# Quarter of the gram evacuation to VectorE, its additions to GpSimd, and another order of loads and weights, in a fused pairwise-interaction MLP

## What is computed

```python
dots = einsum('bfd,bgd->bfg', bottom_output, bottom_output)
pairs = dots[:, TRIL_I, TRIL_J]                 # 351 per sample
x = concatenate([bottom_mlp_output, pairs, zeros], axis=1)     # 480
for w, b in ((w0, b0), (w1, b1), (w2, b2), (w3, b3)):          # 1024, 1024, 512, 256
    x = relu(x @ w.T + b)
return x @ w_out.T + b_out
```

## Time and profile before

| | us |
|---|---|
| median of 3 runs | 570.56 |
| lowest and highest run | 570.14, 571.0 |
| profiled execution, its span from first to last instruction | 570.2 |
| PE busy (share of the span) | 542.0 (95%) |
| ScalarE busy | 340.8 (60%) |
| VectorE busy | 330.0 (58%) |
| GpSimd busy | 10.8 (2%) |

### The profile page before, as it was taken

One profiled execution on the slowest core, in us unless ns is written; L12 is line 12 of the kernel. 1 busy time (PEld: TensorE's weight loads), 2 busy tenths in 40 slices (PEclk: granted clock), 3 DMA queues, 4 the chain that ended last, 5 costly groups with the idle time before them and its releaser, 6 DMA issues.

```text
span 570.2 us, 13265 instructions
## 1 busy us (share of the span) xinstructions
PE 542.0 (95%) x4457; PEld 531.7 (93%) x4457; DVE 330.0 (58%) x941; ACT 340.8 (60%) x900; POOL 10.8 (2%) x58
## 2 busy tenths in 40 slices
PE   4768799999999999999999999999999999999997
PEld 3667799999999999999999999999999999999996
DVE  3778678727872488427872488427872488425222
ACT  4988479827971499317971499417981399414112
POOL 1500000000000000000000000000000000000000
PEclk9977899999999999999999999999999999999999
DMA  7987324044304141232304131222304131200000
GB/s 222 260 233 223 89 65 117 12 104 124 109 16 119 37 121 47 61 87 78 109 11 112 43 116 53 62 87 77 109 7 111 47 115 56 55 22 1 1 1 0
DMA packets 89898, 47.32 MB, mean 83 GB/s; under 512 B 25851, under 2 KB 88083, under 8 KB 89875
## 3 DMA queue, kind: packets, MB, share of 16 engines
q1 hardware_dynamic: 89874, 47.02, 29.5%
HBM read 41.03 MB, written 5.98 MB: 82 GB/s over the span
## 4 chain that ended last, share of the span: by engine, by line
PE 73%; ACT 12%; DMA 6%; issue 5%; SPq 2%; DVE 0%; ACTq 0%; DVEq 0%
PE acc L551 61%; ACT parts L641 9%; PE gram_ps L518 6%; PE turned_ps L502 5%; DMA rows<-in_r_bottom_output_dram 5%; ACT xt L624 2%; ACT h_full L654 1%; DMA blocks<-grams 1%; PE gram_ps L485 1%; SPq L366 1%; SPq L355 1%; SPq L344 1%; DMA pairs<-blocks 1%; PE turned_ps L564 0%; PE turned_ps L527 0%
## 5 line engine op out<-in xcount | busy, mean ns | idle before, releaser
L551 PE MATMUL acc<-h_a,w_hi 128*128 128x256 f32 x1152 | 211.2, 283 | 0.9 <-ACT h_full L654 0.8
L654 ACT ACTIVATE h_full<-acc,small_t 128x256 f32<-128x256 f32 x176 | 83.2, 473 | 183.2 <-PE acc L551 181.5
L551 PEld LDWEIGHTS acc<-h_a,w_hi 128*128 128x128 f32 x1152 | 179.2, 191 | 2.2 <-ACT h_full L654 2.2
L641 ACT ACTIVATE parts<-gram_ps 27x216 f32<-27x216 f32 x512 | 173.4, 339 | 5.9 <-PE gram_ps L518 1.1
L551 PE MATMUL acc<-h_a,w_lo 128*128 128x256 f32 x576 | 163.0, 283 | 0.0
L551 PEld LDWEIGHTS acc<-h_a,w_lo 128*128 128x128 f32 x576 | 110.4, 192 | 0.0
L551 PE MATMUL acc<-x,w_hi 128*128 128x256 f32 (+1 forms) x512 | 98.5, 289 | 3.7 <-DVE x L806 3.7
L518 PE MATMUL gram_ps<-xt 128*128 128x256 f32 x512 | 95.9, 312 | 1.0 <-ACT parts L641 0.7
L551 PE MATMUL acc<-h_b,w_hi 128*128 128x256 f32 x512 | 93.3, 284 | 0.0
L736 DVE TENSOR_TENSOR xt<-turned_ps,xt 128x432 fp32r<-128x432 f32 x128 | 77.3, 604 | 18.7 <-ACT xt L624 15.7
L502 PE MATMUL turned_ps<-ident,rows 108*128 108x108 f32 x512 | 72.8, 267 | 16.0 <-DMA rows<-in_r_bottom_output_dram 15.1
(11 more groups left out here) (54 smaller groups left out, 346.3 us busy)
## 6 DMA issues: line engine op xcount, KB each, us to landing
rows<-in_r_bottom_output_dram SPq DMA_DIRECT2D x128, 216.0 KB
blocks<-grams SPq DMA_DIRECT2D x32, 182.2 KB
stage_b<-in_L_rec_w_dram SPq DMA_DIRECT2D x2, 1024.0 KB, 9.6
stage_b<-in_L_rec_w_dram SPq DMA_DIRECT2D x1, 2048.0 KB, 7.8
stage_a<-in_L_rec_w_dram SPq DMA_DIRECT2D x1, 1536.0 KB, 11.5
stage_pairs<-in_L_rec_w_dram SPq DMA_DIRECT2D x1, 1408.0 KB, 9.7
mlp_rows<-r_bottom_mlp_output_dram SPq DMA_DIRECT2D x8, 128.0 KB, 2.2
pairs<-blocks SPq DMA_DIRECT2D x8, 126.0 KB
```

The source lines that it names most:

```text
L551: last = nc.tensor.matmul(acc_slot(slot), weight(wp, layer, m, k), in_tile(layer, k, xp), start=(k == 0 and n == 0), stop=(k == K_TILES[la ...
L641: last = nc.scalar.activation(parts[quad, u % 2, :, :, 0:FEATS], gram_ps[quad, b:b + GRAM_BANKS, :].rearrange("p a (b h n) -> p h (a b) n" ...
L654: nc.scalar.activation(h_full[:, slot % 2, :], acc_slot(slot), ACT.Relu, bias=small_t[:, slot:slot + 1]).then_inc(drained, 1)
```

## The change

- Of a unit's four quadrant copies ScalarE keeps three (`ACT_QUADS`), VectorE does the fourth (`last_part`). VectorE keeps the 32 by 32 transpose (`turn_low`); GpSimd does both additions (`add_parts`).
- The pairs are held in the order of W0's columns, so no column is moved. The gather has 28 pieces, each of one feature's rows; the DRAM scratch is laid out by quadrant, so the spill writes whole rows of `grams` and a gathered pair row is four runs of 64 numbers. Chunk 0's pieces are issued half by SP and half by ScalarE, after its fifth group of weights; later chunks' all by SP. The pair tiles have a semaphore each.
- The raw weights lie where `w_lo` will be and are split in place. The groups go in the order W0, small, W1, W2, W3. Nine are turned ahead of chunk 0, none of them between units. Chunk 0 has a hook every six matmuls (`FIRST_HOOK`): the first sixteen take W1, then come the units of chunk 1, and from unit 4 on a group of W2 or W3 stands behind each of ten units. These ten use the `turned_ps` bank that the next unit's transposes use, which wait for the group's `w_done`.
- Chunk 0's rows have sixteen places of their own or nearly so (eight share memory with `h_b`, four are the ring, four are used twice), and are loaded with 112 instead of 108 partitions. Ten loads go out ahead of W0.
- Chunk 0's products wait for the groups that they need, tile by tile.

```diff
-BETWEEN_UNITS, FIRST_BETWEEN = 8, 7
+ORDER = W0_ALL + SMALL + W1_ALL + W2_ALL + W3_ALL
+BEFORE_CHUNK, LATE_WEIGHTS = ORDER.index(W1_ALL[0]), ORDER.index(W2_ALL[0])
-HOOK = 9
+HOOK, FIRST_HOOK = 9, 6
+GATHER_AFTER, LATE_FROM = 4, 4
+ACT_QUADS = 3
+def first_hooks():
+    hooks, late = groups(BEFORE_CHUNK, LATE_WEIGHTS), groups(LATE_WEIGHTS, W_GROUPS)
+    for u in range(UNITS + XT_LAG):
+        hooks.append(unit_steps(u))
+        if u >= LATE_FROM and late:
+            hooks.append(late.pop(0))
+    return hooks + late
...
         def weight_bank(n):
-            if n < BETWEEN_UNITS:
-                return acc[:, n % ACC_RING, :]
+            if n >= LATE_WEIGHTS:
+                return turned_ps[:, (LATE_FROM + n - LATE_WEIGHTS + 1) % TURN_RING, :]
             return gram_ps[:, n % (GRAM_RING * GRAM_BANKS), :]
+        def gather_piece(engine, a, b, n, q):
+            dst = pairs[q % P:q % P + n, q // P, :].rearrange("p (s r) -> p s r", s=GROUP)
+            engine.dma_start(dst, pair_rows[a, b:b + n]).then_inc(gathered[q // P], 16)
...
                 for s in range(GROUP):
-                    sp.dma_start(blocks[:, :, s * RUN:(s + 1) * RUN],
-                                 grams[QUAD * s:QUAD * s + FEATS, :, :]).then_inc(spilled, 16)
+                    sp.dma_start(blocks[s], grams[quad_of(s)]).then_inc(spilled, 16)
...
+            for u in range(10):
+                load_early(u)
+            for i in range(2):
+                sp.dma_start(raw_rows(0)[:, 4 * i:4 * i + 4, 0:LAYERS[0][0]], w0_rows[:, 4 * i:4 * i + 4, :]).then_inc(w0_loaded[i], 16)
+                load_early(10 + i)
+            for u in range(12, UNITS):
+                load_early(u)
             load_mlp(0)
...
+            for i in range(2):
+                load_weights(1, w1, 2 * i, 2 * i + 2, w1_loaded[i])
             spill(0)
+            gather(0, PIECES[0::2])
+            for i in range(2, 4):
+                load_weights(1, w1, 2 * i, 2 * i + 2, w1_loaded[i])
             for u in range(ROWS_RING):
                 load_rows(1, u)
+            for i in range(2):
+                load_weights(2, w2, 2 * i, 2 * i + 2, w2_loaded[i])
+            load_weights(3, w3, 0, 2, w3_loaded)
...
-            for col, n, q, step in ROW_RUNS:
-                nc.gpsimd.tensor_copy(w0_ordered[:, :, q:q + (n - 1) * step + 1:step], stage_pairs[:, :, col:col + n])
+            def add_parts(d, u):
+                n = d * UNITS + u + 1
+                hh, hl = parts[:, u % 2, 0], parts[:, u % 2, 1]
+                pool.wait_ge(parts_done, n)
+                pool.wait_ge(last_part_done, n)
+                nc.gpsimd.tensor_tensor(hh, hh, hl, ALU.add).then_inc(sum_done, 1)
+                pool.wait_ge(sum_done, n)
+                pool.wait_ge(low_turned, n)
...
+                nc.gpsimd.tensor_tensor(
+                    grams[:, :, u * UNIT_GROUPS:(u + 1) * UNIT_GROUPS].rearrange("p g j -> p j g"),
+                    parts[:, u % 2, 0, :, 0:FEATS], low_t[:, u % 2, :, 0:FEATS], ALU.add).then_inc(grams_done, 1)
...
             def turn_weights(n):
+                elif n >= LATE_WEIGHTS:
+                    pe.wait_ge(xt_done, UNITS + LATE_FROM + n - LATE_WEIGHTS)
...
             def turn(d, u):
+                if isinstance(d, int) and d == 1 and LATE_FROM < u <= LATE_FROM + W_GROUPS - LATE_WEIGHTS:
+                    pe.wait_ge(w_done, LATE_WEIGHTS + u - LATE_FROM)
...
             def gram_parts(d, u):
-                for s in range(GROUP):
+                for s in range(ACT_QUADS):
+                    last = nc.scalar.activation(parts[quad_of(s), u % 2, :, :, 0:FEATS], gram_found(u, s), ACT.Copy)
                 last.then_inc(parts_done, 1)
...
+            def last_part(d, u):
+                dve.wait_ge(gram_done, d * UNITS + u + 1)
+                for s in range(ACT_QUADS, GROUP):
+                    last = nc.vector.tensor_copy(parts[quad_of(s), u % 2, :, :, 0:FEATS], gram_found(u, s))
+                last.then_inc(last_part_done, 1)
```

More of the change, by code:

```diff
@@ L143, in first_steps, with groups, chunk_steps @@
         steps += unit_steps(u)
[L144 to L163, removed]
+    steps.append(("mlp",))
+    for n in range(BEFORE_CHUNK):
+        steps.append(("weights", n))
+        if n == GATHER_AFTER:
+            steps.append(("gather",))
+    return steps + [("pairs",)]
+def first_hooks():
+    def groups(n0, n1):
+        return [[("weights", n)] for n in range(n0, n1)]
+    hooks, late = groups(BEFORE_CHUNK, LATE_WEIGHTS), groups(LATE_WEIGHTS, W_GROUPS)
[4 more added lines that the diff above has]
+    return hooks + late
+def chunk_steps(gram, first=False):
+    steps, done = [], 0
+    hooks = first_hooks() if first else [unit_steps(u) for u in range(UNITS + XT_LAG)] if gram else []
+    every = FIRST_HOOK if first else HOOK
+    hooks.reverse()
     for layer in range(3):
@@ L176, in chunk_steps @@
                 done += 3 * n
-                if layer < 2 and done % HOOK == 0:
-                    hook()
-                if done == OUT_UNIT * HOOK:
+                if layer < 2 and done % every == 0 and hooks:
+                    steps.extend(hooks.pop())
+                if done == OUT_UNIT * every:
                     steps.append(("out",))
@@ L481, in turn_weights @@
                     if part == 0:
                         pe.wait_ge(loaded, 16)
-                    for k in range(4):
-                        at = (4 * part + k) * P
-                        last = nc.tensor.transpose(bank[:, k * P:(k + 1) * P], src[:, at:at + P], ident[:])
-                last.then_inc(w_turned, 1)
+                src = raw_rows(layer)[:, m, :]
+                for k in range(4):
+                    kk = K_LAST if layer == 0 and k == 3 else P
+                    at = (4 * part + k) * P
+                    last = nc.tensor.transpose(bank[0:kk, k * P:(k + 1) * P], src[:, at:at + kk], ident[:])
@@ new lines, in turn_weights, with turn_rows, turn_early @@
+                last.then_inc(w_turned, 1)
+            def turn_rows(u, src):
+                for j in range(UNIT_GROUPS):
+                    last = nc.tensor.transpose(turned_ps[:, u % TURN_RING, j * GROUP_ROWS:(j + 1) * GROUP_ROWS],
+                                               src[0:GROUP_ROWS, j, :], ident[0:GROUP_ROWS, 0:GROUP_ROWS])
+                last.then_inc(turned, 1)
+            def turn_early(u):
+                pe.wait_ge(early_loaded[u], 16)
+                if u >= TURN_RING:
+                    pe.wait_ge(xt_done, u + 1 - TURN_RING)
+                turn_rows(u, early_rows_of(u))
```

282 lines of the change are left out of this document (126 added, 156 removed).

## The result

| | before | after |
|---|---|---|
| median, us | 570.35 (4 runs) | 583.95 (4 runs) |
| lowest and highest run | 568.98, 571.0 | 583.55, 585.17 |
| profiled execution, span | 570.2 | 581.8 |
| ScalarE / VectorE / GpSimd busy | 340.8 / 330.0 / 10.8 | 305.9 / 325.7 / 115.5 |

The changed kernel takes 1.025 times as long, interval 1.0232 to 1.0268. The forecast was 577.0 in a range of 567 to 589: slower was right, by 6.6 us forecast and 13.6 measured.

A forecast was written before the change was run, and what follows sets the result against it. PE bounds the steady chunks; ahead of chunk 0 it waits for rows and a serial chain to the pairs. 570.2 - 14.3 + 7.7 + 11.5 + 3.4 + 1.0 - 2.4 = 577.1, given as 577.0, range 567 to 589.

The forecast's parts named there:

- The road to the pairs of chunk 0: Ahead of chunk 0: faster units, spill and gather bring the first pairs product to 48.2 from 62.55 us, gain 14.3.
- the two roads to the pairs: Ahead of chunk 0: the gather with the last tile's work, and ScalarE's issues then four weight groups, both end at 48.2.
- rival 1: Chunk 0: ScalarE's and VectorE's copies run ahead of PE, the bank waits' 11.5 us fall away, 565.5 us; chance 0.16.
- rival 2: Gather: pieces cost 0.79 us each, delaying chunk 0, chunk 1 and each later chunk, 610 us; chance 0.08.
- rival 3: First stage: GpSimd's two additions set the pace at about 2.0 us a unit, +6, 583 us; chance 0.12.
- the ten bank waits: Chunk 0: PE waits for turned_ps banks used by W2 and W3 groups, 5 x 0.85 + 5 x 1.45 = +11.5 us.
- the wait before chunk 1: End of chunk 0: PE is through at 89.1, chunk 1's pairs are ready at 92.5, so it waits 3.4 us.
- the start value of the sum: Whole kernel: the sum starts from the profiled span, 570.2 us, with no correction to the median of 570.56.
- chunk 0 without the wait behind it: Chunk 0: 18 more weight groups (+7.7 us) and the bank waits (+11.5) lengthen it from 69.9 to 89.1 us.
- slow clock in chunk 1: Start of chunk 1: a slower PE clock after the wait for its pairs adds 1.0 us.
- five steady chunks and the last: Later chunks: ScalarE's gaps give back 0.4 us in each of six, -2.4 us; bounds 0 and 0.9 each.
- rival 4: Chunks' layer 0: GpSimd and VectorE block each other, 0.25 us over in ten hooks of six chunks, +15, 592; chance 0.05.

The follow-up runs named there:

- experiment 8: Changed kernel with ScalarE's fourteen gather issues for chunk 0 behind all nine groups of W0 and small vectors instead of the first five: 583.34 us.
- experiment 1: Changed kernel with the ten W2 and W3 groups right behind W1's, in the gram banks, and the units of chunk 1 after them: 571.7 us.
- experiment 2: Changed kernel with the ten W2 and W3 groups behind the units of chunk 1, in the gram banks: 567.89 us.
- experiment 4: Changed kernel with both additions back on VectorE, which also keeps the fourth quadrant's copy: 623.59 us.
- experiment 3: Kernel before with only the new division of gram work among ScalarE, VectorE and GpSimd, from chunk 1's grams on: 565.29 us.
- experiment 6: Changed kernel with the early loads of chunk 0's rows on 108 partitions instead of 112: 583.72 us.

## Why the prediction was right and wrong

**Right.** The road to the pairs of chunk 0, all of it by its steps: ScalarE's unit 1.53 to 1.60 us (1.50 forecast), spill issued at 33.6 (34.0), landed 5.2 us later (5.5), pieces at 0.40 from start to start (0.38 in the sums), first product on pairs 48.3 (48.2). In one place the steps may not hold: the forecast let the two roads to the pairs end together, and experiment 8 points to ScalarE's as the later one. GpSimd's additions 0.47 and 0.43 (0.5). PE stood before all of the ten turns named, released by w_lo, and before chunk 1, released by the last pair tile and the drain behind it. Experiments 1 and 2 show that these waits are the loss, and the first of them gives their price: 12.2 us. No rival came about: the fastest bank wait was 0.95 us (rival 1 needed 0.67 on the mean), in chunk 1's gather one piece of 28 took 0.89 us, the first 0.57 and the others 0.24 to 0.42 (rival 2), GpSimd was far under 1.5 us a unit (rival 3).

**Wrong, by 7.0 us.** Every wait stood where it was forecast; the sizes were wrong. The step that failed most is the price of the ten bank waits, put at 11.5 us and measured at 14.0; behind it stand the wait before chunk 1, which came out of a wrong boundary of chunk 0, and the start value of the sum. The ledger runs over the profiled spans, before and after, which differ by 11.5 us where the terms summed to 6.9:

| term | forecast | measured |
|---|---|---|
| start of chunk 0's pairs | -14.3 | -14.23 |
| chunk 0 without the wait behind it | +19.2 | +22.70 |
| wait before chunk 1 | +3.4 | +4.74 |
| slow clock in chunk 1, with what that chunk gains | +1.0 | +1.64 |
| five steady chunks and the last (forecast: six times 0.4) | -2.4 | -3.34 |

1. *The ten bank waits.* "Sum 5 x 0.85 + 5 x 1.45 = +11.5" was 14.0: PE stood 1.56 us the first time, 1.72 to 1.74 in the five with a drain and 0.95 in the other four. Three things add up to the 2.5 us. From VectorE's last result to PE's next start it is 0.15 us (79.04 to 79.19), where the sum had 0.05: 1.0 over ten waits. The first wait, without a drain, had ScalarE still on the unit's three parts: 0.6. And in each of the five with a drain the cast on VectorE, which the subtraction and the weights' rest stand behind, took 0.48 to 0.49 us instead of 0.29, while GpSimd's first addition ran (81.74 and 81.86 in the timeline): that is the 0.9 left. In experiment 4, where GpSimd adds nothing, no cast takes over 0.30. That is 2.5 of the 3.5 us in the second line. Another 0.6 is the half clock: 10.3 us of it around chunk 0's start, 4.6 us of work at half speed inside the chunk and so 2.3 us lost, where the forecast kept the 1.7 of the earlier trace rows. The last 0.4 us has no row of its own.

2. *The boundary of chunk 0.* "Chunk 0 itself takes 69.9 us" was read between 62.2 and 132.1, but chunk 1's first product stood at 130.4: the 132.1 was nine products and a turn into it. In the sum of differences that cancels, except in one place. "PE is through at 89.1, so it waits 3.4" sets one end counted from single durations (92.5) against one counted from the 69.9. With 68.1 PE is through at 87.3 and waits 5.2, and that is 1.8 us more in the sum. The measured 4.7 has two errors that nearly cancel: both the pairs and PE's end came 3 to 4 us later than that.

3. *"The span of the profiled execution is 570.2 us, the median of the runs shown 570.56, nothing worth a correction."* This compared a span with a whole time. In the 22 runs of the kernel before beside experiment 1, the time is 2.5 us longer than the span and the median span is 567.75. So the profiled execution of before was 2.4 us longer than its typical run; the time that belongs to it is 572.7 us, and a start from the median run would have been a start from 567.75 of span. That 570.2 still lay beside the median time is luck: the long execution stood in for the 2.5 us outside the span. Experiment 3 shows where such an execution can lose: its own, with the same work ahead of chunk 0, had the pairs 3.4 us earlier. So the gain of 14.2 in the first line of the ledger hit the forecast against one execution; against 59.11 it would be 10.8. How the median execution of before divides is not shown, since one was traced. The changed kernel's profiled execution is a typical one (span 581.8, time 583.55). Of the 7.0 us missed, 4.8 are the terms and their rounding (a span of 581.8 against 577.0) and 2.2 what was never added: 1.8 outside the span, 0.4 from the profiled run to the median. And of the difference between the two kernels, 13.6 us, the spans of the two profiles show only 11.5, since the one of before lies high.

4. *"Of ScalarE's gaps I count 0.4 us back in each of six."* It was 0.66: the 0.30 at the drain of the earlier trace rows went, as did a smaller gap ahead of a gram behind it and others. This was within the bounds given, and the only term for which the forecast was too slow.

**The rule weighed against the trace.** In the changed kernel the 30 of VectorE's 168 subtractions that overlap a GpSimd addition take 0.52 to 0.67 us instead of 0.43 (which lifts the mean of those that write h_a from 426 to 452 ns), and five casts take 0.48 to 0.49 instead of 0.29, all five in bank waits. The Trainium skill, "SBUF — State Buffer", section "Who interferes with whom", has such an instruction and GpSimd's exclude each other; the trace agrees that they hinder each other, with at most 0.25 us for one instruction. That one waits for the whole of the other it does not show: a subtraction at 223.20 us began with 0.29 us of GpSimd's addition left and took only 0.14 longer. On the mean, 26 ns in 425, that is a small part of rival 4, whose steady chunks would have been slower and were 0.66 us faster; on PE's path it shows in the five bank waits, some 0.9 us in all. The Trainium skill, "DMA: Bandwidth & Descriptors", section "Why a DMA increments its semaphore by 16 and not by 1", would have the loads of 112 rows spread over more engines than those of 108; experiment 6 shows no shorter time from it.

## What to carry to other kernels

When a buffer is lent to a second use, price the lending by the whole path until it is free again, with whatever stands ahead on each engine of that path, and compare it with the work that the lender has in between; if it is short, put the borrowed work where the lender has none, as experiments 1 and 2 did for 12 and 16 us with the same instructions. A change with several parts is worth splitting: the part that moved work to an idle engine paid 5 us by itself, while the earlier start, 14 us between the two profiled executions, was all given back in the next chunk until the order there was mended. And before a forecast adds differences to a profiled execution, it should be known how far that execution's span and whole time lie from the median run.

## What the runs showed of the hardware

- The time outside the span is a property of the kernel: 2.5 us in all 45 runs of the kernel before beside the experiments, 1.8 in the changed one and all its variants, 2.0 in experiment 3.
- PE's clock fell to half (1.2 GHz) at 141.6 us, while PE stood still before chunk 1, and stayed there for 6.8 us, 4.8 of them work; in experiment 2, without that wait, it did not fall there. Executions of one kernel differ in it: ten runs of experiment 1 had spans of 567.6 to 571.9, and the four longest a mean granted clock of 0.973 to 0.976 where the others had 0.977 to 0.982.
- A VectorE subtraction of 128x256 from two SBUF tiles takes 0.52 to 0.67 us instead of 0.43 where it overlaps one of GpSimd's additions (30 of 30 in the changed kernel); without such an overlap it is not slower (138 of 138).
- Small DMAs have a price by the piece on the issuing queue: 28 pieces of 1 to 26 rows took 11.2 us on SP, 14 took 6.2 on ScalarE's queue.
- The spill of the same 729 KB in four DMAs landed 5.2 us after its first issue with whole rows of `grams` as runs, 7.6 with runs of 256 bytes.
